# Attention and mixture of experts: z is split into its high and low part where it is made, not where it is used

## The reference, cut to what matters

```python
q, k, v = [einsum('ihd,bpd->biph', W, x) for W in (W_Q, W_K, W_V)]      # x: 2048 x 512, 16 heads of 128
z = einsum('biqp,biph->biqh', softmax(masked(q @ k.T) / sqrt(128)), v)
x = layernorm(x + einsum('df,bqf->bqd', W_O, z_flat))                    # z_flat: 2048 x 2048
scores = softmax(x @ gate_w.T)                                           # 64 experts, the best 6 of each token
# each expert takes up to 128 of its tokens: silu(xe @ w1.T) * (xe @ w3.T) @ w2.T, weighted by the gate
x = layernorm(x + routed + shared_expert(x))
```

## Time and profile before

| | us |
|---|---|
| median of 3 runs (lowest to highest) | 2666.51 (2664.92 to 2666.80) |
| the profiled execution, its own time | 2663.28 |
| span of the profiled execution | 2661.6 |
| attention, routing, experts, last normalisation | 0 to 1697, 1697 to 1945, 1945 to 2620, 2620 to 2662 |
| TensorE, VectorE, ScalarE, POOL busy | 2489.5, 1778.8, 1460.7, 274.6 |
| mean granted TensorE clock | 0.975 |

### The profile page before, as it was taken

One profiled execution on the slowest core, in us unless ns is written; L12 is line 12 of the kernel. 1 busy time (PEld: TensorE's weight loads), 2 busy tenths in 40 slices (PEclk: granted clock), 3 DMA queues, 4 the chain that ended last, 5 costly groups with the idle time before them and its releaser, 6 DMA issues. The chain is left out here.

```text
span 2661.6 us, 47883 instructions
## 1 busy us (share of the span) xinstructions
PE 2489.5 (94%) x14304; PEld 2153.4 (81%) x14304; DVE 1778.8 (67%) x3809; ACT 1460.7 (55%) x3254; POOL 274.6 (10%) x221
## 2 busy tenths in 40 slices
PE   6999999999999999999999999798899999999992
PEld 5888888888888888888888888576688988898992
DVE  3665566566466557557466566588868887787885
ACT  3555555455456456456455455444437776677772
POOL 0000000000000000000000000045541222221120
PEclk8999999999999999999999999899999999999996
DMA  6311311310320321311221120467659999999995
GB/s 245 122 49 48 118 49 51 117 50 21 104 94 15 107 79 32 106 54 54 85 79 54 67 78 17 151 225 262 226 155 285 313 300 278 287 307 294 287 314 187
DMA packets 178147, 383.77 MB, mean 144 GB/s; under 512 B 19689, under 2 KB 52585, under 8 KB 167600
## 3 DMA queue, kind: packets, MB, share of 16 engines
q1 hardware_dynamic: 155248, 333.38, 37.2%
q0 software_dynamic: 20288, 42.59, 7.2%
q10 hardware_dynamic: 2304, 4.20, 0.4%
HBM read 282.37 MB, written 106.35 MB: 146 GB/s over the span
## 5 line engine op out<-in xcount | busy, mean ns | idle before, releaser
L403 ACT ACTIVATE pT_hi<-turned 128x512 fp32r<-128x512 f32 (+3 forms) x640 | 331.1, 537 | 311.0 <-PE turned L626 309.6
L497 DVE TENSOR_TENSOR pT_lo<-turned,pT_hi 128x512 fp32r<-128x512 f32 (+3 forms) x640 | 376.6, 606 | 100.9 <-ACT pT_hi L403 99.6
L392 ACT ACTIVATE probs<-bank,neg_max 128x512 f32<-128x512 f32 (+3 forms) x640 | 396.0, 626 | 80.7 <-DVE neg_max L491 76.9
L483 DVE TENSOR_REDUCE max_part<-bank 128x1 f32<-128x512 f32 (+2 forms) x576 | 347.6, 622 | 108.0 <-PE bank L609 99.2
L596 PE MATMUL bank<-x_sb,w_hi 128*128 128x512 f32 x1024 | 327.3, 401 | 20.5 <-ACT ident_bf L367 13.8
L626 PE MATMUL turned<-ident,probs 128*128 128x128 f32 x2176 | 323.6, 275 | 19.6 <-issue 19.1
L626 PEld LDWEIGHTS turned<-ident,probs 128*128 128x128 f32 x2176 | 265.4, 142 | 64.8 <-issue 20.6
L641 PE MATMUL z_ps<-pT_hi,v_hi 128*128 128x512 f32 (+3 forms) x640 | 255.2, 399 | 15.7 <-DVE pT_lo L497 12.9
L609 PE MATMUL bank<-k_lo,q_hi 128*128 128x512 f32 (+2 forms) x640 | 254.0, 397 | 0.0
L1756 DVE TENSOR_TENSOR up_lo<-w_raw,up_hi 128x704 fp32r<-128x704 f32 x262 | 222.4, 887 | 42.0 <-ACT up_hi L1256 41.3
L609 PE MATMUL bank<-k_hi,q_hi 128*128 128x512 f32 (+2 forms) x640 | 250.4, 391 | 0.0
(11 more groups left out here) (211 smaller groups left out, 5352.4 us busy)
## 6 DMA issues: line engine op xcount, KB each, us to landing
w_raw<-in_w SPq DMA_DIRECT2D x262, 352.0 KB, 5.6
x_sb<-x_parts SPq DMA_DIRECT2D x62, 1024.0 KB, 6.4
w_raw<-in_w SPq DMA_DIRECT2D x129, 256.0 KB, 5.1
rows_in<-gathered_x SPq DMA_DIRECT2D x65, 263.5 KB, 5.4
gathered_x<-empty_row SPq DMA_DIRECT2D x64, 263.5 KB, 9.2
z_dram<-z_sb SPq DMA_DIRECT2D x64, 256.0 KB, 2.9
z_raw<-z_dram SPq DMA_DIRECT2D x16, 1024.0 KB, 5.6
w_raw<-in_w_qkv SPq DMA_DIRECT2D x32, 384.0 KB, 10.2
```

Of the source, the lines that this page charges most:

```text
L392: nc.scalar.activation(probs[:, u % 2, r, kc * CHUNK:kc * CHUNK + used], bank[:, job_at["s", h, c, r, kc] % BANKS, 0:used], ACT.Exp, bias= ...
L403: nc.scalar.activation(pT_sb[0][:, n % TURNS, lo_col:], turned[:, n % TURNS, lo_col:], ACT.Copy).then_inc(turn_hi, 1)
L483: nc.vector.reduce_max(max_part[:, row % ROWS, kc:kc + 1], bank[:, job % BANKS, 0:used], axis=AX_X).then_inc(part_done, 1)
L497: nc.vector.tensor_tensor(pT_sb[1][:, n % TURNS, lo_col:], turned[:, n % TURNS, lo_col:], pT_sb[0][:, n % TURNS, lo_col:].bitcast(F32), AL ...
```

## The change

ScalarE copies z_sb to a new tile z_high in the step "out", after VectorE's product; VectorE subtracts it from z_sb in place in a new step "zlow", which stands twelve places after "out" in the list of steps (the last one at its end). SyncE stores both parts in the step "zlow". z_dram has both parts, twice the size. In the routing, load_z fetches both parts (2 x 1 MB) straight into the tiles that TensorE reads; split_z is gone on both engines. The load for tile k+1 is issued when the product of tile k-1 is done (out_ready), at the head of SyncE's step k. The row of zeros is 256 floats shorter, so that each of its stores is made in two pieces. z_raw's place stays empty (z_pad0).

```diff
@@ attention_plan
+    for unit in units:
+        place = plan.index(("out", 0, *unit)) + 12
+        plan.insert(min(place, len(plan)), ("zlow", 0, *unit))
@@ attention: tiles, semaphores
+    EMPTY = DM // 2
+        z_hi = sb("z_high", [P, CHUNK], F32R)
-        empty_row = sb("empty_row", [P, ROW], F32)
+        empty_row = sb("empty_row", [P, ROW - EMPTY], F32)
+        zhi_out = sem("zhi_out")
+        zhi_done = sem("zhi_done")
+        zlo_done = sem("zlo_done")
@@ attention, SyncE
-                            sp.dma_start(gathered_x[bass.ds(e, 1)].rearrange("a p n -> (a p) n"),
-                                         empty_row[:]).then_inc(zero_out, 16)
+                            empty = gathered_x[bass.ds(e, 1)].rearrange("a p n -> (a p) n")
+                            sp.dma_start(empty[:, 0:EMPTY], empty_row[:, 0:EMPTY]).then_inc(zero_out, 16)
+                            sp.dma_start(empty[:, EMPTY:], empty_row[:]).then_inc(zero_out, 16)
...
-                    if step[0] == "out":
+                    if step[0] == "zlow":
                         _, _, h, c = step
                         u = unit_at[h, c]
-                        dst = z_dram[c * RPC:(c + 1) * RPC, :, bass.ds(i * 2 + h, 1), :].rearrange("t p a n -> p (t a) n")
-                        sp.wait_ge(z_done, upto(i, n_units, u))
-                        sp.dma_start(dst, z_sb[:, u % 2].rearrange("p (t n) -> p t n", n=P)).then_inc(z_out[u % 2], 16)
+                        dst = [z_dram[part, c * RPC:(c + 1) * RPC, :, bass.ds(i * 2 + h, 1), :].rearrange("t p a n -> p (t a) n")
+                               for part in range(2)]
+                        sp.wait_ge(zhi_done, i * n_units + (u + 1))
+                        sp.dma_start(dst[0], z_hi[:].bitcast(F32).rearrange("p (t n) -> p t n", n=P)).then_inc(zhi_out, 16)
+                        sp.wait_ge(zlo_done, i * n_units + (u + 2))
+                        sp.dma_start(dst[1], z_sb[:, u % 2].rearrange("p (t n) -> p t n", n=P)).then_inc(z_out[u % 2], 16)
...
-            sp.dma_start(sums_dram[SEQ:SEQ + P], empty_row[:, 0:DM]).then_inc(zero_out, 16)
+            for first in range(0, DM, EMPTY):
+                sp.dma_start(sums_dram[SEQ:SEQ + P, first:first + EMPTY], empty_row[:, 0:EMPTY]).then_inc(zero_out, 16)
@@ attention, ScalarE
+            def result_high(i, h, c):
+                u = unit_at[h, c]
+                act.wait_ge(z_done, upto(i, n_units, u))
+                act.wait_ge(zlo_done, i * n_units + (u + 1))
+                act.wait_ge(zhi_out, i * (16 * n_units) + 16 * (u + 1))
+                nc.scalar.activation(z_hi[:], z_sb[:, u % 2], ACT.Copy).then_inc(zhi_done, 1)
...
+                    if step[0] == "out":
+                        result_high(i, *step[2:])
@@ attention, VectorE
+            def result_low(i, h, c):
+                u = unit_at[h, c]
+                dve.wait_ge(zhi_done, i * n_units + (u + 1))
+                nc.vector.tensor_tensor(z_sb[:, u % 2].bitcast(F32R), z_sb[:, u % 2], z_hi[:].bitcast(F32),
+                                        ALU.subtract).then_inc(zlo_done, 1)
...
+                    if step[0] == "zlow":
+                        result_low(i, *step[2:])
@@ route_and_experts, SyncE
             def load_z(i, k):
-                sp.dma_start(z_raw[:], z_dram[bass.ds(i * NB + k, 1)].rearrange("a p h n -> (a p) h n")
-                             ).then_inc(z_in, 16)
+                for part in range(2):
+                    sp.dma_start(z[part][:, k % 2].bitcast(F32), z_dram[part, bass.ds(i * NB + k, 1)].rearrange("a p h n -> (a p) h n")
+                                 ).then_inc(z_in[k % 2], 16)
...
-            sp.wait_ge(z_lo, 1)
             load_z(0, 1)
...
             def step(i, k):
+                if exists(i, k - 1) and exists(i, k + 1):
+                    sp.wait_ge(out_ready, done(i, k - 1))
+                    load_z(i, k + 1)
...
-                if exists(i, k + 2):
-                    sp.wait_ge(z_lo, done(i, k + 1))
-                    load_z(i, k + 2)
@@ route_and_experts, TensorE
-                    pe.wait_ge(z_lo, done(i, k))
+                    pe.wait_ge(z_in[k % 2], i * (32 * NB // 2) + 32 * (k // 2 + 1))
@@ route_and_experts: split_z goes, on ScalarE and VectorE, with its calls in step and ahead of the first tile
-                nc.scalar.activation(z[0][:, k % 2], z_raw[:], ACT.Copy).then_inc(z_hi, 1)
...
-                nc.vector.tensor_tensor(z[1][:, k % 2], z_raw[:], z[0][:, k % 2].bitcast(F32),
-                                        ALU.subtract).then_inc(z_lo, 1)
@@ the memory between the two
-    z_dram = dram("z_dram", [TILES, P, HEADS, P])
+    z_dram = dram("z_dram", [2, TILES, P, HEADS, P])
```

More of the change, by code:

```diff
@@ L262, in _ @@
             pool.wait_ge(const_step, 3)
-            nc.gpsimd.iota(empty_row[:, TOKEN:TOKEN + 1].bitcast(I32), pattern=[[0, 1]], base=SEQ,
+            nc.gpsimd.iota(empty_row[:, TOKEN - EMPTY:TOKEN - EMPTY + 1].bitcast(I32), pattern=[[0, 1]], base=SEQ,
                            channel_multiplier=1).then_inc(pool_const, 1)
@@ L307, in _ @@
                 sp.sem_inc(z_out[n], 8 * n_units)
+            sp.sem_inc(zhi_out, 16)
             zeroed = {1: range(0, 3), 2: range(3, 6), 3: range(6, 8)}
@@ L340, in _ @@
             body(PAIRS - 1, True)
-            sp.dma_start(sums_dram[SEQ:SEQ + P], empty_row[:, 0:DM]).then_inc(zero_out, 16)
+            for first in range(0, DM, EMPTY):
+                sp.dma_start(sums_dram[SEQ:SEQ + P, first:first + EMPTY], empty_row[:, 0:EMPTY]).then_inc(zero_out, 16)
             sp.wait_ge(x_in, 32 * (CHUNKS * PAIRS - 1))
-            sp.wait_ge(zero_out, 16 * (EXPERTS + 1))
+            sp.wait_ge(zero_out, 16 * (2 * EXPERTS + DM // EMPTY))
+            sp.wait_ge(zhi_out, 16 * (n_units * PAIRS + 1))
             for n in range(2):
@@ L447, in _ @@
             dve.sem_inc(z_done, n_units)
+            dve.sem_inc(zlo_done, 1)
             def split_w(i, dt):
@@ L797, in route_and_experts @@
             wo = [sb(f"wo_{n}", [P, HEADS, DM], F32R, first) for n in ("hi", "lo")]
-            z_raw = sb("z_raw", [P, HEADS, P], stack=first)
+            z_pad0 = sb("z_pad0", [P, HEADS, P], stack=first)
             z = [sb(f"z_{n}", [P, 2, HEADS, P], F32R, first) for n in ("hi", "lo")]
@@ L886, in route_and_experts @@
         gw_in = sem("gw_in")
-        z_in = sem("z_in")
+        z_in = [sem(f"z_in{n}") for n in range(2)]
         x_in = [sem(f"xr_in{n}") for n in range(2)]
-        z_hi = sem("z_hi")
-        z_lo = sem("z_lo")
         out_ready = sem("out_ready")
@@ L1146, in _ @@
                 if k == TILES - 2:
-                    sp.wait_ge(z_hi, done(0, TILES - 1))
-                    sp.wait_ge(z_lo, done(0, TILES - 1))
                     for t in range(2):
@@ L1237, in step @@
                     exponentials(i, k - 2)
-                if exists(i, k + 1):
-                    split_z(i, k + 1)
                 if exists(i, k - 1):
@@ L1339, in body @@
                         split_piece(i, q)
-            split_z(0, 0)
             for g in range(HEADS // GROUP):
@@ L1610, in split_wo @@
                                         ALU.subtract).then_inc(wo_split, 1)
-            def split_z(i, k):
-                dve.wait_ge(z_hi, done(i, k))
-                nc.vector.tensor_tensor(z[1][:, k % 2], z_raw[:], z[0][:, k % 2].bitcast(F32),
-                                        ALU.subtract).then_inc(z_lo, 1)
             def normalise(i, k):
```

## The result

| | kernel before | changed kernel |
|---|---|---|
| median of 5 runs each, side by side (us) | 2664.92 | 2680.62 |
| lowest to highest | 2658.33 to 2666.80 | 2673.23 to 2697.23 |
| the profiled execution, its own time | 2663.28 | 2673.23 |
| span | 2661.6 | 2671.8 |

The ratio is 1.0072, 95% interval [1.0053, 1.0092]: slower by 0.7%. The forecast was 2671, with 2654 to 2690 around it. It had the sign and was too low by 10 us on the median. As a change it was lower still, +4.2 us for a measured +15.7, since the kernel before ran at 2664.92 in this set and the forecast was built on 2666.51. A second set of runs (e1) gave 1.0076 [1.0060, 1.0093].

The account below looks back on a forecast made before the run. TensorE was taken to bound attention and experts, DVE with z_lo the routing. Terms 9.2 + 1.9 + 3.0 + 0.5 - 10.4 = +4.2 us on the 2666.5 median gave 2671, range 2654 to 2690.

Parts of the forecast that it names:

- Attention, +9.2: Attention: the added copy and subtraction stall TensorE at two units, 1.15 us per pair of heads, times 8, +9.2 us.
- The stall of 0.7 us at unit (0,2): Attention, head 0, chunk 2: a low part ends at 589.1 where TensorE takes it at 588.41, a 0.7 us stall.
- 0.45 at (1,2): Attention, head 1, chunk 2: a low part ends at 614.4 where TensorE began at 613.97, a 0.45 us stall.
- unit (1,1): Attention, head 1, chunk 1: among the units said to have room for both added steps, with no stall.
- End of the attention, +1.9: After the last product: ACT's copy, DVE's subtraction and one more issue of zeros all on the path, +1.9 us.
- Start of the routing, +3.5: Routing start: one more MB of z ahead of w_o, 3.0 us, plus 0.5 booked for z of tile 1.
- The pace, 14.3: Routing: tiles at 14.3 us, midway between POOL's 14.7 and DMA's 13.9, for 15.04 before; -10.4 us over 14 tiles.
- The release of POOL: Routing: with z_lo gone from DVE, POOL gets back an estimated 1.0 us per tile.
- POOL would run at 14.7: Routing: POOL's chain of scatter, landing, weight split and next load falls from 15.7 to 14.7 us per tile.
- the second rival's smaller price: Routing: second megabyte delays each scatter by two thirds of 3.0 us; POOL 16.7 per tile, total 2683; rival's chance 0.20.
- The sign that I had written down for it: Routing: POOL's waits for landings going from 3 to 6 us to 6 to 9 would show that scatters are delayed.
- the hand-over: Routing to experts: expert 0's rows load after the last scatter lands, about 9 of 14.6 us slack; no change booked.

Follow-up runs that it names:

- e1: The changed kernel run again with no edit, against the kernel before: ratio 1.0076 [1.0060, 1.0093].
- e7: The kernel before, with POOL's shared-piece subtraction and next piece's load moved ahead of its wait for the scatter's landing: ratio 1.0006 to the kernel before.
- e5: The changed kernel, with the routing loading only z's high part per tile and the low part's tile set to zero: ratio 0.9935 to the kernel before.
- e4: The changed kernel, with POOL's shared-piece subtraction and next piece's load moved ahead of its wait for the scatter's landing: ratio 0.9992 to the kernel before.

## Why the prediction was right in sign and too low

**Attention, +9.2.** Mechanism right, size too low. The stall of 0.7 us at unit (0,2) was measured as 0.74, but up to the next z_sb another 0.4 joined it; 0.45 at (1,2) was 0.60; and the 0.40 up to unit (1,1) lies where I had written that there was room. The fixed part is 2.1 us for 1.15 in seven pairs and 1.2 in the last (2.6 in e1), 16 to 18 us in all. The step that failed: I followed only the low parts that TensorE's products with v wait for, and not ScalarE's exponentials, behind which the banks for the next scores come free (the new wait for probs above). That this wait is what joined the stall is read from the views; no run tests it alone. As the pairs' starts happened to be closer by 0.5 to 1.2 us, and the first z_sb came 1.6 and 3.3 us earlier, 7 to 11 us of it were seen in the two profiles of the changed kernel, and 13.8 between the means of all with either attention. So the term was too low by some 5 us.

**End of the attention, +1.9:** 1.66. **Start of the routing, +3.5:** w_o's first split came 9.9 us after the first load for 7.8, 2.1 later and not 3.0; but tile 1's product began 25.08 us after the first load where it was 24.87, since it had waited for its z before as well. I had added the lateness of w_o to that of z of tile 1; only the later of the two counts.

**The pace, 14.3.** This is the step that failed, in its sign as well: -10.4 us forecast, +3.6 and +9.9 measured. Its ground was right: e7 shows VectorE as the bound before, e5 gives 13.2 for the split alone. The release of POOL came too: its subtraction of 128x704 takes 1.74 us in the mean for 2.17, each of the six scatter issues 1.00 for 1.116, 1.1 us per tile together where I had 1.0. What was wrong is "POOL would run at 14.7", which kept the wait for the landing as it was. It grew by 2.0 us, and POOL went from 15.7 to 16.7 per tile (tile 1 at 1779.90, tile 11 at 1947.38). That is the second rival's smaller price to the tenth, and its 2683 is nearer to the median of 2680.6 than my 2671; it had 0.20. The sign that I had written down for it came as well, landing waits of up to 8.5 us for 6.9. I had used DMA's mean share as the bound and not asked what a load, on its way when the scatter is issued, does to that scatter. And the rival had its place wrong: I let the delay show only at the hand-over, with 9 us of slack. It shows in every tile, through ACT's order of work. SyncE asks for expert 0's rows 289.1 us after the first load of z, 285.3 before.

**The total.** It lies in my range in part by luck. The range was 36 us wide, the sign came from the attention and the two starts, and the pace, which should have taken most of that back, had the wrong sign.

**Ports and queues.** With z_lo gone from DVE, POOL's subtraction fell from 2.17 to 1.74 us. The rule on the exclusive lock in the Trainium skill (SBUF — State Buffer, "SBUF: two separate sides") agrees with that. On POOL's queue, beside twice the load of z, the scatters landed 2.0 us later and the loads of the shared piece took 7.8 us (median) for 4.3. The Trainium skill (DMA: Bandwidth & Descriptors, "Queues, rings and completion order") states that each engine goes round the queues packet by packet; that does not mean a cheap sharing here.

## What to carry to other kernels

Before work is taken off an engine that sets the pace, write down the next chain with every wait in it, and ask of each whether the bytes that the change adds make it longer. Where an engine issues a load, look at what it waits for first: a wait that nothing in the load needs belongs behind it, and such a fix is worth nothing until the bound above it is gone (e7: no change, e4: 0.8%, the same edit). Where a view names the engine that ended a wait, look whether what it made had long been ready; in e4 it had, and the wait was for a landing. In a full order of steps, an added step is to be checked against all that TensorE waits for, the banks that come free as well as the operands.

## What was not expected of the hardware

A stall of TensorE costs more than its own length. The changed kernel in stretches of 4 us around the long wait above (the column behind the five engines is the granted clock):

```profile
1850.00:1854.00 4.00, 2.40 (x11) 1.66 (x9) 0.00 (x0) 0.00 (x0) 3.08 (x4) 1.00 0.96 305
1854.00:1858.00 4.00, 0.00 (x0) 0.00 (x0) 0.00 (x0) 1.68 (x2) 1.58 (x2) 0.70 1.01 400
1858.00:1862.00 4.00, 1.44 (x6) 1.34 (x7) 2.61 (x13) 2.60 (x6) 0.73 (x1) 0.50 0.39 145
1862.00:1866.00 4.00, 3.53 (x11) 2.33 (x10) 3.79 (x8) 0.80 (x2) 3.09 (x4) 0.52 0.41 110
1866.00:1870.00 4.00, 4.00 (x23) 3.38 (x23) 3.33 (x11) 2.07 (x2) 3.09 (x4) 1.00 0.78 306
```

While TensorE stood for 8 us, the clock fell from 1.00 to 0.50 (1.2 GHz for 2.4) and was back only for the stretch from 1866. Over the whole stretch it is 0.94 for 0.98 before. In the 5 us that TensorE worked between 1858 and 1866, half the speed cost some 2.5 us, an estimate from these rows, for each long tile. And 1.05 MB more per tile cost 2.1 to 2.5 us in one order of POOL's work, while with two lines of it moved the same bytes ran only 0.35 us above the pace without them.
